# Opening of a two-layer transformer kernel: Newton steps of two batches and two weight low parts moved to VectorE, ScalarE's opening reordered

## What is computed

```python
ln_out = _ln(hidden_states, ln_w, ln_b)                 # rows of x, normalised
q  = _fp8_linear_pertensor(ln_out, wq, ...)             # clip(x/scale), round to fp8, matmul
q  = _ln(q, qln_w, qln_b)                               # per head of 128
k  = _ln(_fp8_linear_pertensor(ln_out, wk, ...), ...)
v  = _fp8_linear_pertensor(ln_out, wv, ...)
core = _gqa(q, k, v)                                    # softmax(q k / sqrt(128)) v
qx = _ln(_fp8_linear_pertensor(ln_out, wqx, ...), ...)
kx, vx = split(cond @ w_kv_x); kx = _ln(kx, ...)
xout = _gqa(qx, kx, vx)
out = fp8(cat(core, xout) / proj_smooth) @ wproj
```

## Time and profile before

| | before |
|---|---|
| median of three runs | 846.38 us |
| runs | 848.02, 845.90, 846.38 us |
| the profiled execution, its own time | 851.64 us |
| its span (first to last instruction) | 849.7 us |
| busy: TensorE matmul, VectorE, ScalarE, GpSimd | 789.4, 659.8, 539.0, 469.3 us |
| instructions: VectorE, ScalarE, GpSimd | 1563, 1236, 786 |
| granted TensorE clock, mean | 0.981 |

### The profile page before, as it was taken

The page is one execution under the profiler, slowest core; times in us unless marked ns, Lnnn a source line. Parts: engine busy times, 40 slices in busy tenths (PEclk is TensorE's granted clock), DMA queues, the critical chain, the costliest instruction groups (busy, mean ns, idle before and its releaser), DMA issues.

```text
span 849.7 us, 14340 instructions
## 1 busy us (share of the span) xinstructions
PE 789.4 (93%) x4848; PEld 675.2 (79%) x4848; DVE 659.8 (78%) x1563; ACT 539.0 (63%) x1236; POOL 469.3 (55%) x786
## 2 busy tenths in 40 slices
PE   3677999999999999999899999999999999798998
PEld 3466788888888888888788878998888877577787
DVE  6889988899888998889789795965554689966534
ACT  5889777788777886788675555433332278874332
POOL 2698959769687896859845576342210016970000
PEclk9899999999999999999999999999999999899999
DMA  7000120011200121000200323977421010100001
GB/s 239 14 0 1 38 75 1 2 39 38 76 1 1 39 66 47 2 2 1 68 25 14 114 76 81 235 185 248 131 64 49 1 45 14 50 14 0 1 1 51
DMA packets 28264, 45.59 MB, mean 54 GB/s; under 512 B 3936, under 2 KB 18080, under 8 KB 28064
## 3 DMA queue, kind: packets, MB, share of 16 engines
q1 hardware_dynamic: 26800, 41.31, 16.7%
q10 hardware_dynamic: 1392, 3.37, 1.1%
HBM read 43.49 MB, written 1.18 MB: 53 GB/s over the span
## 4 chain that ended last, share of the span: by engine, by line
PE 60%; DVE 20%; ACT 8%; issue 4%; POOL 4%; DMA 3%; SPq 0%; ACTq 0%; DVEq 0%
PE PS L771 16%; PE PS L841 7%; PE PS L726 6%; PE PS L631 6%; PE PS L700 4%; PE PS L662 4%; PE PS L952 2%; PE PS L672 2%; PE PS L683 2%; DVE cat L1543 2%; PE PS L653 2%; DMA l_KM<-share 2%; POOL raw L2217 2%; PE PS L710 2%; DVE yb L1539 1%
## 5 line engine op out<-in xcount | busy, mean ns | idle before, releaser
L2217 POOL TENSOR_SCALAR raw<-raw,mvq,rsq 128x128 f32<-128x128 f32 x312 | 186.6, 615 | 1.6
L771 PE MATMUL PS<-xq,WH 128*128 128x512 f32 x472 | 148.3, 396 | 1.0 <-ACT l_x2T L996 1.0
L771 PEld LDWEIGHTS PS<-xq,WH 128*128 128x128 f32 x472 | 86.3, 190 | 18.1 <-issue 2.1
L631 PE MATMUL PS<-WH,xq 128*128 128x256 f32 (+1 forms) x256 | 89.2, 366 | 7.0 <-DVE xq L1543 6.1
L771 PE MATMUL PS<-xq,WL 128*128 128x512 f32 x236 | 92.5, 392 | 0.0
L631 PE MATMUL PS<-WL,xq 128*128 128x256 f32 (+1 forms) x256 | 85.1, 350 | 0.0
L1110 ACT ACTIVATE P<-PS,sm 128x256 f32<-128x256 f32 x128 | 60.8, 494 | 29.5 <-DVE sm L1701 29.3
L1637 DVE BATCH_NORM_STATS2 st<-raw 128x6 f32<-128x128 f32 x320 | 72.0, 277 | 2.0 <-ACT raw L1082 2.0
L841 PE MATMUL PS<-xq,m_hh 128*128 128x256 f32 x384 | 69.7, 282 | 0.9 <-DVE m_hl L1993 0.7
L700 PE MATMUL PS<-PT,vr 128*128 128x256 f32 x256 | 68.0, 389 | 2.2 <-ACT PT L996 2.1
L726 PE MATMUL PS<-PH,cat 128*128 128x256 f32 x256 | 65.0, 293 | 5.3 <-DVE cat L1543 5.3
(11 more groups left out here) (301 smaller groups left out, 2192.4 us busy)
## 6 DMA issues: line engine op xcount, KB each, us to landing
wst<-in_wgu SPq DMA_DIRECT2D x24, 256.0 KB, 3.7
l_KM<-share SPq DMA_DIRECT2D x16, 384.0 KB, 4.4
wst<-in_wall SPq DMA_DIRECT2D x18, 256.0 KB, 3.1
l_KM<-share SPq DMA_DIRECT2D x16, 256.0 KB, 5.5
dst<-in_wdn SPq DMA_DIRECT2D x24, 128.0 KB, 3.1
wst<-in_wkvx SPq DMA_DIRECT2D x8, 256.0 KB, 3.2
l_KM<-share SPq DMA_DIRECT2D x16, 128.0 KB, 4.5
m_pre<-in_wo ACTq DMA_DIRECT2D x1, 2048.0 KB, 10.4
```

What stands on the lines that cost most here:

```text
L631: t = e.matmul(PS[:, b, o:o + n], xq[s][:, k, c * 128:(c + 1) * 128], W[:, k, w0:w0 + n], start=(k == 0 and i == 0), stop=(k == 1 and i == 1))
L771: t = e.matmul(PS[:, b, :], W[wi][:, gu, k, :], a[:, k, cols], start=(n == 0), stop=(n == 5))
L2217: t = e.tensor_scalar(v, v, mvq[:, par, n, 0:1], rsq[:, par, n:n + 1], ALU.add, ALU.mult)
```

## The change

`newton` runs on VectorE for steps 0 and 1, inside `begin_q`, with the mean's factor and, for step 0, `nmq`; GpSimd's `norm_q` keeps only the scale-and-add there. WL of pieces 4 and 5 is made on VectorE (`load_first`). On VectorE `ln_rest_stats` and `ln_rest` move behind quantise(1). On ScalarE pieces 5, 2 and 3 are loaded earlier, div(2) moves behind the evictions of part 1, and `norm_a` and the evictions of part 0 of chunks 2 and 3 move ahead of centre(3) and div(4). On TensorE `ln(1)` moves behind part 1 of batch 0.

```diff
@@ attention_order
     for q in range(3):
         for c in range(2):
             do("p1", 0, c, PARTS[q])
-        if q == 1:
-            do("ln", 1)
+    do("ln", 1)
     do("vx", 0)
@@ scalar
             load_w(0, 4)
+            load_w(0, 5)
             div(0)
-            load_w(0, 5)
             load_w(0, 0)
             div(1)
             load_w(0, 1)
+            load_w(0, 2)
             take_kx(0)
             for c in range(2):
                 take_p1(0, c, PARTS[0])
-            load_w(0, 2)
+            load_w(0, 3)
             for c in range(2):
                 take_p1(0, c, PARTS[1])
-            load_w(0, 3)
             centre(1)
-            div(2)
             for c in range(2):
                 take_p1(0, c, PARTS[2])
+            div(2)
             centre(2)
             div(3)
             for c in range(2, 4):
                 take_p1(0, c, PARTS[0])
             take_vx(0)
+            norm_a()
+            for c in range(2, 4):
+                take_p1(0, c, PARTS[1])
             centre(3)
             div(4)
-            for c in range(2, 4):
-                take_p1(0, c, PARTS[1])
-            norm_a()
             for c in range(2, 4):
                 take_p1(0, c, PARTS[2])
@@ vector: begin_q
-                e.tensor_scalar(y.bitcast(I32), y.bitcast(I32), -1.0, float(0x5F3759DF), ALU.mult, ALU.add).then_inc(roots.sem, 1)
+                i = e.tensor_scalar(y.bitcast(I32), y.bitcast(I32), -1.0, float(0x5F3759DF), ALU.mult, ALU.add)
+                if s > 1:
+                    i.then_inc(roots.sem, 1)
+                else:
+                    i.then_inc(dv.sem, 1)
+                    yield from newton(v, y, dmq[:], dv.up())
+                    e.tensor_scalar(m, m, -0.5, None, ALU.mult).then_inc(roots.sem, 1)
+                    if s == 0:
+                        w.wait_ge(roots.sem, roots.at[0])
+                        e.tensor_tensor(nmq[:], m, y, ALU.mult).then_inc(rooted_q, 1)
@@ vector
+            def load_first(j):
+                src, o = staged(("w", 0, j))[0], slice(j * 256, (j + 1) * 256)
+                w.wait_ge(w_hi.sem, w_hi.at[0, j])
+                e.tensor_tensor(WL[:, :, o], src[:], WH[:, :, o].bitcast(F32), ALU.subtract).then_inc(w_lo_d.sem, 1)
@@ vector: the opening
-            weave(ln_rest_stats())
-            weave(quantise(0))
-            rest = ln_rest()
-            for c in range(6):
-                next(rest)
-            weave(quantise(1))
-            weave(rest)
+            for j in (4, 5):
+                load_first(j)
+            weave(quantise(0))
+            weave(quantise(1))
+            weave(ln_rest_stats())
+            weave(ln_rest())
             weave(chain(*[lambda c=c, q=q: stats(0, c, PARTS[q]) for q in (0, 1) for c in (0, 1)]))
@@ gpsimd: norm_q
-                newton(mvq[:, par, :, 1], rsq[:, par, :], ntq[:, :])
-                e.tensor_scalar(mvq[:, par, :, 0], mvq[:, par, :, 0], -0.5, 1.0, ALU.mult, ALU.mult).then_inc(po.sem, 1)
-                w.wait_ge(po.sem, po.up())
-                if s == 0:
-                    e.tensor_tensor(nmq[:], mvq[:, 0, :, 0], rsq[:, 0, :], ALU.mult).then_inc(rooted_q, 1)
+                if s > 1:
+                    newton(mvq[:, par, :, 1], rsq[:, par, :], ntq[:, :])
+                    e.tensor_scalar(mvq[:, par, :, 0], mvq[:, par, :, 0], -0.5, 1.0, ALU.mult, ALU.mult).then_inc(po.sem, 1)
+                    w.wait_ge(po.sem, po.up())
@@ gpsimd
-            for j in (4, 5, 0, 1, 2, 3):
+            for j in (0, 1, 2, 3):
                 load_w(0, j)
```

More of the change, by code:

```diff
@@ L486, in program @@
         scaled_x = count("scaled_x", range(4))
-        w_lo = count("w_lo", [(0, j) for j in WORDER] + [(gp, j) for gp in range(1, 4) for j in WORDER[:3]])
-        w_lo_d = count("w_lo_d", [(gp, j) for gp in range(1, 4) for j in WORDER[3:]])
+        w_lo = count("w_lo", [(0, j) for j in WORDER[2:]] + [(gp, j) for gp in range(1, 4) for j in WORDER[:3]])
+        w_lo_d = count("w_lo_d", [(0, 4), (0, 5)] + [(gp, j) for gp in range(1, 4) for j in WORDER[3:]])
         p_hi = count("p_hi", [(gp, p) for gp in range(4) for p in range(4)])
```

## The result

The changed kernel took **860.14 us**, the median of 4 runs (858.94 to 862.43), against 847.2 us of the kernel before in the same session (4 runs, 845.9 to 848.76): a ratio of 1.0144, 95% interval 1.0116 to 1.0172. It is slower, as forecast. A second measurement of the same code, made with the experiments, gave 858.34 us (5 runs, 856.09 to 861.29) against 848.3 (11 runs), ratio 1.0105 with 1.0074 to 1.0136. The forecast of 855.9 us on a base of 846.4 is a ratio of 1.0112. The ratios are the recorded ones; the quotients of the medians are a little higher, 1.0153 and 1.0118.

The account below looks back on a forecast made before the run. The opening was taken as a chain over all engines up to step 1's transpose, TensorE bounding from 60 us on. The steps' delays reached plus 9.6, taken as +9.5, on the 846.4 median: 855.9 us, range 849.0 to 859.5.

Parts of the forecast that it names:

- Step A: VectorE's opening up to centre(1): three meetings with GpSimd and the moved statistics put centre(1) at 28.0, plus 1.3 us.
- B: From centre(1) to quantise(2): two evictions now stand before div(2), taking 4.3 us; plus 0.5, in all +1.8.
- C: Up to the end of quantise(3): 11 new small VectorE instructions in begin_q(0) add 2.2 us, ending at 44.2.
- Step D: Up to quantise(4): div(4) behind the part-0 evictions makes a 7.5 us round trip; start 51.7 instead of 42.39, +9.3.
- F: Up to the first maximum on VectorE: ten new small instructions in begin_q(1), 2.0 us; it comes at 62.0.
- G: quantise(5) loses its 0.53 us wait for div(5) and ends at 66.1; TensorE's product starts at 66.3.
- Step H: Handover: GpSimd in time, TensorE's eight products at the lower clock take 3.77; step 1's transpose at 70.1, plus 9.6 us.
- E: VectorE's 1.04 us wait for norm_a and the eviction behind it goes, bringing the delay to +8.3.
- Recovery behind 60 us: Rivals: TensorE's later waits absorb delay; the partial case shrinks it to 3.9 us, 850.3 us, chance 0.15.
- full recovery: Rival: all 7.4 us of TensorE's waits from 60 to 130 us are used, +2.1, 848.5 us; chance 0.07.
- The faster case: Rival: norm_a off the path and shorter Newton steps give -3.7, 842.7 us, if div(4) is ready by 46.4; chance 0.10.
- all downward bounds at once: Sum's lower corner: no GpSimd meetings (2.5 less) and faster TensorE pace twice (up to 1.7 each) give +3.8.

Follow-up runs that it names:

- e7: The e1 kernel with the low parts of pieces 4 and 5 back on GpSimd; 851.97 us in one run.
- e1: The changed kernel with centre(3) and div(4) back ahead of norm_a and the part-0 evictions of chunks 2 and 3; 851.21 us, ratio 1.0038 to the kernel before.
- e2: The kernel before with only centre(3) and div(4) moved behind the part-0 evictions of chunks 2 and 3 on ScalarE; 852.17 us, ratio 1.0038.
- e3: The kernel before with only the Newton steps of steps 0 and 1 moved to VectorE; 851.13 us, ratio 1.0025.
- e12: The changed kernel, unaltered, in another execution; 858.34 us, ratio 1.0105 to the kernel before.
- e11: The kernel before with the Newton steps on VectorE and the changed ScalarE order from centre(3) on, without the opening edits; 856.97 us, ratio 1.0102.
- e4: The changed kernel with the Newton steps of steps 0 and 1 back on GpSimd; 858.38 us, ratio 1.0105 to the kernel before.

## Why the prediction was right, and where it was not

The direction and the mechanism held, and each step came within 0.4 us of its time on record. The forecast was worked on a load of weights at 8.99 us; in the profile of after it stood at 8.34, so 0.65 is to be taken off every time on record before it is compared:

| step | on record | less 0.65 | measured |
|---|---|---|---|
| A: quantise(0) starts | 13.1 | 12.45 | 12.28 |
| A: quantise(1) ends | 22.6 | 21.95 | 22.07 |
| A: centre(1) | 28.0 | 27.35 | 27.30 |
| B: quantise(2) starts | 32.3 | 31.65 | 31.40 |
| C: quantise(3) ends | 44.2 | 43.55 | 43.55 |
| D: quantise(4) starts | 51.7 | 51.05 | 51.00 |
| F: first maximum | 62.0 | 61.35 | 60.95 |
| G: quantise(5) ends | 66.1 | 65.45 | 65.39 |
| G: TensorE's product | 66.3 | 65.65 | 65.54 |
| H: transpose of step 1 | 70.1 | 69.45 | 69.09 |

**Step A.** The three meetings with GpSimd are the rows at 14.39, 17.14 and 18.65: 2.17, 1.48 and 1.43 us, where undisturbed ones take 1.23, 0.43 and 0.43. They cost 0.94, 1.05 and 1.00, taken as 0.95 each. The rule of the Trainium skill (SBUF — State Buffer, "SBUF: two separate sides"), a lock for a whole instruction, agrees in kind: L1529 ended at 18.62, 0.29 after GpSimd's instruction of 17.05 to 18.33. The 1.3 us that I allowed for a full block were not reached: GpSimd's instruction had already begun when VectorE's did (at 17.05 and 17.14), so less of it was left, and the one that met the row at 14.39 itself took 1.70 us instead of 1.28. That the low parts cost VectorE nothing under ScalarE's cover is right too (0.69 us each, as estimated); e7 moved them back and the opening stayed.

**Steps B and C** were each off by 0.2, in opposite directions. From centre(1) to quantise(2) it took 4.10 where 4.3 was taken; the row at 31.40 shows no wait, because VectorE's own list reached it just as div(2) ended (29.44 + 1.93 = 31.37). From quantise(2) to the end of quantise(3) it took 12.15 where 11.9 was. The 11 small instructions, at 0.215 us from start to start, account for 0.05 of that (2.25 from 37.53 to 39.78, against 2.2); quantise(3) itself, 3.77 from start to end against 3.60 before, for 0.17.

**Step D** is the loss. The round trip was put at 7.5 us and is 7.46. e1 shows it by taking it away (8.6 of the 9.6 us at the marker go, 2.0 of them by the clock level behind it), e2 by adding the wait alone, at 7.45.

**Steps E to G.** The waits of 1.04 and 0.53 went, as said. The maximum came 0.4 earlier than forecast, quantise(5) took about as much longer.

**Step H** was the least sure. The eight products ran at the lower level, as taken, and GpSimd was in time. They took 3.55 us up to the transpose; the 3.77 of the forecast counts the last product to its end, which is 3.75 here (65.54 to 69.29), while the transpose starts before it. In e1, where TensorE had not been idle so long, they took 1.92, so this term was worth about 1.6 us. The sum of 9.6 was for the transpose of step 1, which moved by 69.09 - 60.50 = 8.59, 9.24 aligned; the marker behind it moved by 9.60.

**The rivals.** Recovery behind 60 us did not come: +9.60 at the first marker is +9.92 at the second, in the second execution +9.34 and +8.33, aligned. The stretch between the markers takes 316.2 us before and 316.6 and 315.2 after, where full recovery would have made it 7.4 shorter. The faster case falls by its own condition: div(4) was ready at 50.97 and not by 46.4. The gain from the Newton steps' shorter chain does exist, as the 1.96 us at 60.50 that e3 and after win back; it is smaller than what VectorE pays for it.

**What was off** is the size in the timed runs, by a little. The first session gave 1.44%, 12.2 us on 846.4; the second gave 1.05%, 8.9 us. The sum says 9.5, and stands between them. On the base of the forecast these are 858.6 and 855.3 us, both inside the range; the first session's own median, on a base of 847.2, is 0.6 above its upper end. No term of the sum failed, but I took the width of the range from the bounds of the steps alone, with nothing for the scatter of the runs (and all downward bounds at once give +3.6 by their own terms, not +3.8). That the shift at the marker agrees with the sum to a tenth is in part luck: the forecast was for the transpose of step 1, 9.24 aligned. The kernel before ran from 845.1 to 853.08 in the last session alone, and from the second marker to the end of the span it takes 472.5 in one profile, while the changed kernel takes 471.4 and 474.7 in its two. What makes that scatter is not shown; the clock level differs between executions at many places, but no run here holds it fixed.

## What to carry to other kernels

In an in-order list, moving a piece behind another puts it behind everything that piece waits for: before div(4) goes behind an eviction, ask whether the product to be evicted is itself waiting for the consumer of the step before. Price such a loop by its whole round trip (here 7.5 us for 2.9 us of work), count the slack behind it once, for all edits together, and add what TensorE loses by its lower clock level after the idle time that the loop leaves it (2.0 of 8.6 us here). And read shifts of a few microseconds from a marker shared by both profiles, aligned at their first instruction, since the ends scatter by as much as the effect.

## What the runs showed of the hardware

TensorE's two levels fall differently on the same instructions in two executions of one program: products of 128x512 at 22 us took 0.39 and 0.63 us, those of 128x256 at 35 us 0.28 and 0.41, with granted clocks of 0.83 and 0.91 as the mean of the first 60 us. Up to the first maximum this changed the pace by nothing in these two executions; in e7 it went with 2.3 us of longer waits.

At one place the level followed the kernel and not the execution: the eight products of step 1. In the four profiles in which VectorE waited over 7 us for div(4) and the first maximum came at 59.4 us or later (after, e12, e11, e4), seven of the eight took 0.63 us each; TensorE had run nothing but one group of scores in the 4.5 to 7.2 us before. In the ten others they took 0.39 to 0.40. The profiles do not show what it takes for the level to change.

The start of the work against the start of the span varies as well: ScalarE's first instruction, behind a DMA, began between 5.95 and 7.09 us over the 14 profiles. That is larger than the effect of some of the edits above.

A dependent chain of small VectorE instructions on 128x20 elements goes at 0.215 us from start to start, with durations of 0.18:

```profile
37.53 0.18 DVE L1602 TENSOR_TENSOR dmq<-rsq 128x20 f32<-128x20 f32 x1
...
39.68 0.18 DVE L1684 TENSOR_TENSOR nmq<-mvq,rsq 128x20 f32<-128x20 f32 x1
```
